# A two-layer decoder block on one core: moved VectorE set-up work, a junction by tiles, and an ending in written-out orders

## What is computed

```python
x = x + L0_attn(ln(x))          # 16 heads of 128, causal, ALiBi
x = x + L0_xattn(ln(x), ctx, mask)  # 16 heads of 16 over 1500 context tokens, then a LayerNorm
x = x + L0_ffn(ln(x))           # ternary weights, int8-like activations, a Hadamard transform
x = x + L1_attn(ln(x))          # 16 heads, tokens as batch: the 8 sequences attend to each other
x = x + L1_xattn(ln(x), ctx)    # decay scan over ctx: only its mean is used; a LayerNorm
x = x + L1_ffn(ln(x))           # round, clip, gelu
```

## Time and profile before

| | us |
|---|---|
| median of 3 runs (610.89 to 612.2) | 611.8 |
| the profiled execution: its own time | 608.25 |
| its span, first to last instruction | 606.3 |
| lead-in and heads 0 to 2 | 50.9 |
| heads 3 to 15, up to the last head's L592 | 117.2 |
| rest of the last head, to the end of its L947 | 11.1 |
| junction, to the first `scores` | 13.4 |
| pairs 0 to 47, to the start of pair 47's `scores` | 313.0 |
| pair 47 and the ending | 100.7 |
| PE busy / DVE busy / ACT busy | 533.7 / 332.6 / 296.3 |

### The profile page before, as it was taken

How to read it: one execution, slowest core, us unless ns; L and a number is a source line. 1 busy time by engine, 2 the same in 40 slices (tenths; PEclk the granted TensorE clock), 3 DMA queues, 4 the chain that set the end, 5 groups by cost and what they waited for, 6 DMA issues and landing times.

```text
span 606.3 us, 16089 instructions
## 1 busy us (share of the span) xinstructions
PE 533.7 (88%) x7056; PEld 413.7 (68%) x7056; DVE 332.6 (55%) x722; ACT 296.3 (49%) x512; POOL 6.4 (1%) x12
## 2 busy tenths in 40 slices
PE   3999878999977999999999969999969998557977
PEld 2577566677755888887888757888747887325635
DVE  3144556454344545475856684755793847763661
ACT  1354552533414666667566536657556556132413
POOL 1000000000011000000000000000000000000000
PEclk9999999999979999999999989999999999879999
DMA  8721211211420121211121101111101100000000
GB/s 287 298 66 42 69 36 36 69 47 60 139 88 0 37 71 36 71 36 37 36 62 43 37 11 35 62 36 36 36 2 36 44 3 10 1 1 1 8 1 8
DMA packets 10743, 30.83 MB, mean 51 GB/s; under 512 B 1329, under 2 KB 4402, under 8 KB 9906
## 3 DMA queue, kind: packets, MB, share of 16 engines
q1 hardware_dynamic: 10482, 29.30, 14.8%
q0 software_dynamic: 192, 0.51, 0.3%
HBM read 29.35 MB, written 0.46 MB: 49 GB/s over the span
## 4 chain that ended last, share of the span: by engine, by line
PE 67%; DVE 17%; ACT 9%; issue 6%; DMA 1%; ACTq 0%; DVEq 0%
PE psb L996 9%; PE psb L1006 9%; PE psa L1031 6%; PE psa L932 6%; PE psb L1049 5%; PE psa L940 5%; PE pst L947 4%; PE pst L1197 3%; PE psb L976 2%; PE pst L1206 2%; PE psa L1257 2%; PE psa L956 1%; ACT shared L504 1%; ACT shared L294 1%; PE psb L967 1%
## 5 line engine op out<-in xcount | busy, mean ns | idle before, releaser
L1006 PE MATMUL psb<-wkv,cx 128*125 128x256 f32 x552 | 80.1, 296 | 10.8 <-ACT kx L345 10.7
L996 PE MATMUL psb<-cx,wkv 128*128 128x500 f32 x288 | 78.8, 410 | 3.5 <-ACT vmem L352 3.5
L1006 PEld LDWEIGHTS psb<-wkv,cx 128*125 128x125 f32 x552 | 70.7, 192 | 15.4 <-ACT kx L345 13.8
L996 PEld LDWEIGHTS psb<-cx,wkv 128*128 128x128 f32 x288 | 51.3, 191 | 16.6 <-ACT vmem L352 4.4
L294 ACT ACTIVATE shared<-shared,negmax 112x112 f32<-112x112 f32 x64 | 24.0, 376 | 71.6 <-DVE negmax L597 71.6
L703 DVE TENSOR_SCALAR shared<-shared,top 125x896 f32<-125x896 f32 x48 | 30.8, 683 | 50.7 <-ACT shared L504 50.5
L352 ACT ACTIVATE vmem<-psb 125x512 f32<-125x512 f32 x46 | 27.4, 595 | 62.3 <-PE psb L1006 62.3
L1031 PE MATMUL psa<-qb,kx 32*125 32x112 f32 x1536 | 54.7, 279 | 1.6 <-issue 1.6
L1031 PEld LDWEIGHTS psa<-qb,kx 32*125 32x125 f32 x1536 | 46.2, 183 | 10.8 <-issue 5.8
L932 PE MATMUL psa<-xnT,whd 128*128 128x448 f32 x128 | 53.1, 559 | 0.0
L703 DVE TENSOR_SCALAR smem<-smem,top 125x896 f32<-125x896 f32 x48 | 30.8, 683 | 40.7 <-ACT smem L504 40.7
(11 more groups left out here) (206 smaller groups left out, 783.4 us busy)
## 6 DMA issues: line engine op xcount, KB each, us to landing
ring<-ctx_t_dram SPq DMA_DIRECT2D x24, 500.0 KB, 3.4
whd<-heads_dram SPq DMA_DIRECT2D x16, 385.0 KB, 3.2
whd<-heads_dram SPq DMA_DIRECT2D x16, 129.0 KB, 2.2
wraw<-w_dram SPq DMA_DIRECT2D x2, 1024.0 KB, 6.2
mats_sb<-mats_dram SPq DMA_DIRECT2D x1, 1536.0 KB, 16.0
wraw<-gate_dram SPq DMA_DIRECT2D x1, 1024.0 KB, 9.9
wraw<-up_dram SPq DMA_DIRECT2D x1, 1024.0 KB, 12.0
wraw<-down_dram SPq DMA_DIRECT2D x1, 1024.0 KB, 13.7
```

Of the source, the lines that this page charges most:

```text
L996: last = nc.tensor.matmul(bank[:, 0:UT], wkv[a][:, 0, c, m * P:(m + 1) * P], cx[b][u % 2][:, c, :], start=(a == b and c == 0), stop=(a == ...
L1006: last = nc.tensor.matmul(bank[0:CT, t * D:(t + 1) * D], cx[b][u % 2][:, c, a0:a0 + CT], wkv[a][:, 1, c, :], start=(a == b and c == 0), st ...
```

## The change

- **One-off work.** It becomes a function `prepare(h)`, called inside `head(h)` behind L603 and ahead of `move_v` (L585) and L610. The ternary weights move from heads 5 to 7 to heads 8 to 10, L655 from 8 to 11, `remainder` of units 0 and 1 from 9, 10 to 12, 13. On PE the bias rows of the first projection (L921) move behind the first head's q, k and v.
- **Junction by tiles.** Tile 0 alone is normalised, transposed and projected before the first `scores`; tiles 1 to 3 do it in pairs 1 to 7 (`normalise1`, `finish1`, `turn_x1`, `project_q`, `spread_q`, with `root(1, t)` and `move_xnT` on ACT). The LayerNorm offset moves from GpSimd to DVE (`add_beta`, pairs 2 to 8).
- **Pairs.** On DVE the order is now `clip`, `take_raw`, late steps, `weigh`. Steps 14 and 15 move to 16 and 17. The last reduction of `attend` (L808) becomes a tree of additions, `gather`. `gu` is computed behind `xq`.
- **Ending.** Behind pair 47 each engine has its own written-out order; banks of PSUM that the pairs no longer use take some results, so that waits for a free bank go; in tile 3 the last gelu is split in two and its table is loaded early.

Core of the diff:

```diff
-                if 5 <= h < 8:
-
-                    n = h - 5
+                if 8 <= h < 11:
+
+                    n = h - 8
...
+                prepare(h)
+                if h + 1 < H0:
+                    move_v(h + 1)
+
+                dve.wait_ge(s_o, h + 1)
...
-            link(nc.vector.tensor_tensor(xs_flat, xs_flat, pst[0:TT, :, :], ALU.add))
-            normalise(1, xs, xn)
+            normalise1(0)
+            finish1(0)
+            spread_q(0)
...
-                nc.vector.tensor_reduce(out=acc, in_=prod[:, 0:n * D].rearrange("p (b e) -> p e b", e=D), axis=AX.X, op=ALU.add).then_inc(s_acc, 1)
+            def gather(t):
+                if t == 3:
+                    link(nc.vector.tensor_tensor(prod[:, 0:4 * D], prod[:, 0:4 * D], prod[:, 4 * D:8 * D], ALU.add))
+                if t == 2:
+                    link(nc.vector.tensor_tensor(prod[:, 0:2 * D], prod[:, 0:2 * D], prod[:, 4 * D:6 * D], ALU.add))
+                if t >= 1:
+                    link(nc.vector.tensor_tensor(prod[:, 0:2 * D], prod[:, 0:2 * D], prod[:, 2 * D:4 * D], ALU.add))
+                nc.vector.tensor_tensor(acc, prod[:, 0:D], prod[:, D:2 * D], ALU.add).then_inc(s_acc, 1)
...
-                if o == 14:
+                if o == 16:
                     add_summary(t)
-                if o == 15:
+                if o == 17:
                     normalise7(t)
...
-                if o == 14:
+                if o == 16:
                     add_normalised(t)
...
-                if o == 14:
+                if o == 16:
                     root(6, t)
...
-                if o == 14:
+                if o == 16:
                     root(7, t)
...
+            for s in range(PAIRS):
+                if s % 2 and s // 2 + 2 < B * UPB:
+                    remainder(s // 2 + 2)
+                if s in (1, 3, 5):
+                    normalise1(s // 2 + 1)
+                if s in (3, 5, 7):
+                    spread_q(s // 2)
                 for t in reversed(range(NT)):
                     early(t, s - 12 * (t + 1))
-                if s < PAIRS:
-                    clip(s)
-                    weigh(s // 2, s % 2)
+                clip(s)
+                if s % 6 == 0 and s:
+                    take_raw(s // 6 - 1)
+                if s in (1, 3, 5):
+                    finish1(s // 2 + 1)
+                if s in (2, 4, 6, 8):
+                    add_beta(s // 2 - 1)
                 for t in reversed(range(NT)):
                     late(t, s - 12 * (t + 1))
+                weigh(s // 2, s % 2)
+                if s % 6 == 5:
+                    keep_weighted(s // 6)
```

The ending on ACT and on DVE, and the last part of it on PE:

```diff
+            move_ctxT(3)
+            root(2, 3)
+            root(3, 3)
+            move_aT(2)
+            move_xqT(3)
+            root(5, 2)
+            silu(3)
...
+            take_raw(7)
+            divide(3)
+            attend(2)
+            centre_delta(3)
+            add_delta(3)
+            quantise(3)
+            gather(2)
+            add_proj(2)
+            times_up(3)
...
+            add_summary(2)
+            scale_hidden(3)
+            add_normalised(2)
+            quantise_hidden(3)
...
+            keep_warm(10)
+            project_hidden(2)
+            keep_warm(16)
+            turn_attended(3)
+            project_attended(3)
+            keep_warm(22)
+            turn_x7(3)
+            hidden(3, 0)
+            hidden(3, 1)
+            keep_warm(3)
+            project_hidden(3)
```

More of the change, by code:

```diff
@@ L514, in _ @@
                     late(t, s - 12 * (t + 1))
+            move_ctxT(3)
[5 more added lines that the diff above has]
+            silu(3)
+            back()
+            move_hT(3)
+            root(6, 2)
+            move_y2(3)
+            root(7, 2)
+            move_xq2T(3)
+            move_x7T(2)
+            root(4, 3)
+            move_h(2, 0)
+            move_tw(3)
+            move_h(2, 1)
+            move_qkv(3)
+            move_xbe(3)
+            gelu(2)
+            back()
+            move_sy(3)
+            softmax_exp(3)
+            move_aT(3)
+            root(5, 3)
+            root(6, 3)
+            root(7, 3)
+            move_x7T(3)
+            nc.scalar.preload_act_table(ACT.Gelu_apprx_tanh)
+            for half in range(2):
+                move_h(3, half)
+            for half in range(2):
+                act.wait_ge(s_hq, 7 + half)
+                nc.scalar.activation(hz[:, half, :], hz[:, half, :], ACT.Gelu_apprx_tanh).then_inc(s_hg, 1)
         @block.vector
@@ new lines, in _, with normalise1 @@
+            move_v(0)
+            for h in range(H0):
+                head(h)
+                if h == 2:
+                    dve.wait_ge(s_tot, 1)
+                    link(nc.vector.tensor_scalar(wmean[:, :], PS[1][:, 1, 448:451], 1.0 / (FF * D), EPS, ALU.mult, ALU.max))
+                    nc.vector.reciprocal(wscale[:, :], wmean[:, :]).then_inc(s_wr, 1)
+            dve.wait_ge(s_y, H0)
+            def normalise1(t):
+                nc.vector.tensor_tensor(xs[:, t, :], xs[:, t, :], pst[0:TT, t // 2, (t % 2) * D:(t % 2) * D + D], ALU.add).then_inc(s_xs1, 1)
+                dve.wait_ge(s_xs1, t + 1)
+                moments(1, t, xs[:, t, :])
```

290 lines of the change are left out of this document (169 added, 121 removed).

## The result

| | before | after |
|---|---|---|
| median of 4 runs (lowest to highest) | 611.35 (609.49 to 612.2) | 590.33 (588.46 to 591.29) |
| the profiled execution: its own time | 608.25 | 590.13 |
| its span | 606.3 | 588.3 |
| mean granted clock of TensorE | 0.972 | 0.959 |

The ratio is 0.9656, with a 95% interval of 0.9623 to 0.969: 21.0 us faster. The forecast was 584.4 with a range of 577 to 592.

A forecast was written before the change was run, and what follows sets the result against it. PE bounds the kernel (busy 88%), so gains come only where it idles, runs at half clock or loses work. Terms -11.4 - 1.0 - 15.9 + 10.0 - 1.0 - 8.1 = -27.4 give 580.9 profiled, 584.4 predicted as median; range 577 to 592.

The forecast's parts named there:

- the ring: Odd pairs with a late step: `weigh` 2.6 to 3.5 later, covered by Hadamard products, 0; uncovered up to 2.5 each.
- the ending: Behind pair 47: waits go and tile 3's chain runs earlier, -8.1; -5 if one more wait of 3 us appears.
- Heads: Heads 3 to 15: one-off work moves into DVE's gap ahead of `move_v`, -11.4; bounds -11.9 and -9.
- The bias rows: L921 in the first projection: they only change places in a stretch where PE is busy anyway, 0.
- Junction: Heads to pairs: first `scores` 5.1 earlier, 3.6 back in pairs 2, 4, 6, ring +0.5; -1.0 in sum.
- The stall of pairs 26 and 27: Steps 14 moved to 16 remove root(7)'s wait for DVE: -8.35, and -7.55 in pairs 38 and 39; -15.9.
- Pair 28: Two table loads ahead of `move_vu`, PE waits some 4.1, then half clock: +5.0, twice with pair 40, +10.0.
- the drain: Skill page's 1.38 us beside each load would make the kernel 5.5 us slower than forecast; left out; chance 0.05.
- Rival 1: The ring decides: late refill in six odd pairs, uncovered 2.5 each, +15, about 598; chance 0.07.
- -10 at full clock: Bound of the ending's term: -10 instead of -8.1 if PE runs at full clock there.
- Late steps ahead of `weigh`: Pairs: PE's waits of a few tenths each for `quantise_hidden` and `take_raw` go, -1.
- Wrong signs named: Any head over 9.5, a stall over 3 us in a pair without one now, or pair 28 to 30 under 14.

The follow-up runs named there:

- The experiment: Against the changed kernel (590.3), the one-off work `prepare(h)` put back behind `head(h)`; measured 598.0, ratio 0.9802.
- The fillings: More multiplications that nobody reads in the ending's PE pauses, against the kernel with `weigh` first in odd pairs and root(6) ahead of silu (570.34); measured 566.22.

## Why the prediction was right, and where its steps failed

The time lies in the range, 1.7 below its upper end, and the sign was sure. The forecast was 5.9 too low, and that it was no more is in part luck. Its sum promised 9.4 more than came (-27.4 against -18.0), mainly by two steps, the ring (8.2) and the ending (2.8), while 1.8 came unforeseen in the lead-in. So it expected 580.9 for the profiled execution, which took 590.13. Then it added 3.5, because the profiled execution before the change lay 3.5 below its median; after the change that distance is 0.2, and so the addition covered a third of the miss.

- **Heads.** Right. All heads from 5 on take 8.78, head 4 takes 8.97 where 9.2 was forecast. The experiment adds that 10.0 of the gain are the place in the head; the text had put all of it to that.
- **The bias rows, "0".** Wrong by itself: PE is busy there, but at half clock. The eight products took 3.72 in front of head 0 and take 1.98 behind v. "Busy anyway" does not say at which clock. In the median it does not show, since the clock takes most of it back at the last head.
- **Junction.** The -5.1 to the first `scores` is right in sum, by two terms. From the end of the last head's projection to `scores` it is 7.7 instead of 13.4, -5.7 (8.3 was forecast); the last head itself is 0.6 longer, its product with v at half clock (2.04 for 1.41). The 3.6 that come back in pairs 2, 4, 6 are 3.1 of PE work (6.2 instead of 5.17 each where the ring is not late), and the ring costs 1.9 there, not 0.5.
- **The stall of pairs 26 and 27.** Right, -8.0 and -7.2 for -8.35 and -7.55; with the steps back the stall is back.
- **Pair 28.** Right in each part: two loads, a wait of 4.06 for the 4.1, half clock behind it (L1100 2.85), 16.79 and 17.45 for the 17.4. On the drain the run decides: in the timeline above, ACT's Ln starts 0.01 after the load's end. The Trainium skill (ScalarE: Activation LUTs, "What ACT_TABLE_LOAD costs") has 1.38 us of drain beside each load. The traces do not agree: wherever an activation did not wait for its input, the load began within 0.03 us of the end of the one ahead, and the one behind began within 0.1 after it. On the number of loads the Trainium skill (the same page, "Table sets: the hidden batching unit") is right about the tables: behind one load of the set that has both, Ln and Exp ran without another. But the list as built has two where the code names no set.
- **The ring, "covered, 0".** This is the step that failed. Pair 18, where I traced it, is covered as I said (6.38 against 6.34 before), though `round_up` waits 2.35. I then took that one pair for all six. Pairs 30 and 42 carry step 18 of an older tile beside step 6 of the younger, so that `move_x7T` stands behind `round_up`, and PE's `turn_inter` waits for it. In pairs 30 and 31 the late ring cost 5.0, in 42 and 43 3.2. The list of odd pairs with a late step also lacked those of `add_down` (21, 33, 45). Behind 21 it costs: in pair 22 `move_tw` stands behind `round_up`, PE's L1267 waits 0.94 for it, and the pair takes 8.26 for 7.08, up to 11.32 in other runs; pair 34 is unchanged. Rival 1 had the mechanism, priced at 2.5 behind each of six odd pairs (its time should read 599.4: 584.4 and 15). It cost nothing behind 17, 19 and 31, nor behind 43, after which nothing is refilled, and 5.0 and 3.2 behind the other two, about half of it the clock.
- **Ending.** -5.3 for -8.1. Up to the second `gate_up` the steps hold, counted from pair 47's `scores`: `turn_context` 3.95 earlier (4.1), `turn_xq` 8.0 (7.9), `gate_up` 7.2 (7.1). Then `times_up` starts 1.6 earlier, not 2.6: the second `gate_up`, which it waits for, took 1.74 where it took 1.07 before, and the forecast names the half clock only for the first. Behind it tile 3's `turn_attended` is 3.6 earlier (5.2), and the last feed-forward, from its first `hidden` on, won 1.9 (2.9), with `hidden` at 3.75 and 2.62. The fillings show that the size of these terms was in the main the clock. One execution does not fix them: nine other profiled kernels with this same ending took 94.6 to 97.1 (95.40 here). The bound of "-10 at full clock" was sound: with more fillings and nothing else the ending is 9.0 shorter than before the change.
- **Late steps ahead of `weigh`, "-1".** Right in sum, by two terms: pairs 12, 20, 32, 36 and 44 gain 2.2, and pair 22 loses 1.2 to the ring.
- **Wrong signs named.** None came true to the letter. The nearest was a new stall of over 3 us in a pair; pair 30 is 2.75 longer and pair 31 2.2, each under that line, and with pairs 42 and 43 it is 8.2. In the run with the bias rows back, whose pairs are the same code, pair 22 is 4.0 longer than before the change.

## What to carry over

A transfer that becomes late is priced by who stands behind its reader in that engine's list, and this must be read in every place where the pattern falls, not in the first one: overlapped tiles put other work behind the same wait. Where an instruction releases a refill, keep it early in just the pairs where it releases one, and let other work pass it in the others. A pause of PE is to be priced twice, once as itself and once for the half clock that may follow it, and where nothing could be done about the pauses, cheap products in four of them paid for themselves (4.1 in all).
